# A four-layer attention network on one core: the causal layer's batches as one list of events, and two full layers in another order

## The chip, the cores and the metric

The kernel runs on one core of one Trainium2 chip. The metric is the device time of one execution in microseconds. The kernel before takes 1417.38 us (median of three runs, 1416.2 to 1417.79).

## The reference

The input x has four batches of 256 channels by 1024 tokens (32x32), all in fp32. It goes through four attention layers one behind the other, each with a residual.

```
x = L0(x)   # 4 batches: softmax(q k) over 1024 keys, q and k of 32 channels, values of 256; gamma * out + x
x = L1(x)   # group norm, q/k/v projections, softmax over 1024 keys, output projection, + x
x = L2(x)   # causal: layer norm, 8 heads of 32 channels over one shared k/v, output projection,
            # layer norm, then feed-forward: ln, w1, ln, gelu, w2, + residual
x = L3(x)   # as L1
```

L0, L1 and L3 are called full layers below, L2 the causal layer. Batches don't depend on each other; within a batch the layers do.

## The kernel before

One program holds two chains of work that share the engines. The full chain runs the twelve full layers in the order of the list `FULL` (L0, L1 and L3, four batches each). The causal chain runs L2 for batches 0 to 3. C0 to C3 are the causal layer of batches 0 to 3 here, L1.2 is L1 of batch 2.

Each chain is a generator on each engine, and the strings in `ORDER` say for each engine which chain takes the next step: digits, letters and F/C. On TensorE a digit (full) or a small letter (causal) also names the PSUM bank where the next unit is put. So the order of the work on each engine is written out by hand or by a search ahead of time, and each engine waits in that order.

Full layer: after the group norm (step gn: a small matmul, L756, then `h_hi` on ScalarE, `h_lo` on VectorE) come the queries q0 (L766), values, and for each of eight query tiles the scores (s, L685 or L716), the row maximum and 1/sum on VectorE, the exponents on ScalarE (L1045), the turned probabilities (t, 4 transposes each, L729, copied by ScalarE at L1058), and four value products o0 to o3 (L738). Product o2 needs turns up to t11, o3 up to t15. VectorE adds the result to the batch's tile (L1312).

Causal layer of one batch: opening (xt transposes of the input, L879; layer norm on VectorE with a root on GpSimd; xn transposes, q2, kv, vt; DMAs that stack q; max products, L951; shift, L908), then eight blocks of exponents (L968) and values (L987) with feed-forward pieces between them, then the rest: w2 of part 2 and all of part 3 (wo, ln2b, f1b, ta, w1, f2b, tg, w2). Feed-forward part 3 is a chain in which each piece needs the one ahead of it. Before the change `causal_schedule` lists these events for a single batch and each engine loops over the batches, so no event of batch b+1 can stand ahead of the last one of batch b:

```python
    tail = NQ - 2
    events += divide + pending + norm(K - 1) + [("tg", tail), ("w2", tail)]
    return events + [(e, tail + 1) for e in FEED_FORWARD]
```

Tiles are shared. Batch tiles are `x[0]`, `x[1]`, `x[0]`, `z` for L0 of batches 0 to 3, and `z`, `x[1]`, `x[0]`, `z` for L3. So the input of batch 3 (`z`) is loaded only when both stores of L3.0 have landed: SyncE issues store, store, load in that order (`stores`, L589; load L580), and its DMAs for the causal chain stand between them in one queue.

Of the kernel before, what the change touches and what calls it, by code (L numbers as in the profile page):

```python
# [8 lines left out]
ALU = mybir.AluOpType  # L9
# [3 lines left out]
P = 128  # L13
# [21 lines left out]
FULL = [("L0", 0), ("L1", 0), ("L0", 1), ("L1", 1), ("L0", 2), ("L3", 0), ("L1", 2), ("L0", 3), ("L1", 3), ("L3", 1),  # L35
        ("L3", 2), ("L3", 3)]
# [8 lines left out]
        "0Fc4F60F2Fe50F72d5F401F760FFF3F516F021FFF3F0215ga1FFF027FFF03F513F5F0246F012F405F710FFF2F456F012FFF3F5670b3F"  # L45
        "FF457FFFac4F6F0ce5F0F2h4F670F234gFahc601hFaFF4cgacFg7a6c0F457gcFcaefFcaFf1F3705gCgbegbCdhaC6fbdFaCfFcaFcCe76"
        "h6aFfFhabCceCbFhdfCbgda6fb1F3hfCC1dC6fCFb2eFgeC6bddC1fa3ahc5dFa7dC05hbFd7C03bCFfa7C56dhaFdCFadFahfc0cCFec624"
        "dFdCC6a23CeCFgCFaFbC3fCFac75a6d4C7aCFgFdCFaC76fC3CFCeFcFCa6F3F15F3Fh0c5F730FecCfd725F017FdFF5F20db3Fh156FFF2"
        "F701efec70bFhFFfcaeh67c6aFFhecaheFcaeaCbg0hgcCehaC1adFf3dCa5dfdC1F5dFh0ceh5c0dC4gFaC360Feh36ehC4aFgc0b67ecFF"
        "agCFC4cCFa7C62aF04f7fFcCeFcFcCe6acFef0123g4acFCgFhFa2C4dC4FgaFCFcga4gCca4F6ca6e1gFdC5Fbd3hfC1C3gC1dFC76f3CFb"  # L50
        "275FdCb7C34acFfhFCFaC3fF7a6C0FdC576aCFCCFhfF1FCa34706FhFFh017FgfFFCca6F4F2a6F4F2ah4F620Fd764F076bcaeFhFhF1F0"
        "7dfdfbca4F76da2aedgFaeFfF0F7eCcf34cf6aCchaC5FFgbdFaCg2d2adC2FfhFaFdedcCfaCecgaCebgdea2hgCCe0FC6cC4a6beFaC4aF"
        "ggCe0cgef6ca6aC2Fega74C0gCFc74cC2aeFgaC4g5a6cheFacCFeaF2egCCaFCeC60b4CgFc6C01eCcgFeFhCcCFa4bCFaCh3C72C0Cbf7F"
        "FFCg707FFFg7a3Fcb53Cfc0F4F6c04ch0Fc345F701F340fgbcFFbFh4F0cg1cgeca5Fhcace7aca10fFFhCdbF4agbCFahgC6320be6ceCa"
        "bFdbCFFdha52dhgaC7ebCdaFbfCdFafcdaFgfCCdChC0bf3Fa5aC5d0fFdC5Facch0ge2ac4C0hcF75dCcC3F750Fc475cCaeFcaCFcageca"
        "gCaFc6F23abCCaCfChCacCfCahc4F601cCdCafCcCaCFCCagFF4FCh63271FaFFa760FbcFFC74F026F4F0264F012F704F617FFF2F014F6"
# [36 lines left out]
NORM_PIECES = 3  # L93
LN_SLOTS = 4
# [63 lines left out]

def causal_schedule():

    events = [("xt", 0), ("xt", 1), ("xn", 0), ("q2", 0), ("kv", 0), ("vt", 0)]
    events += max_events(0) + max_events(1) + [("shift", 0), ("shift", 1)]
# [60 lines left out]
def causal_units():  # L223

    out = [("prep.vo1", "dve", 2), ("prep.qk1", "dve", 1), ("prep.b2", "dve", 1), ("prep.vo3", "dve", 2),
           ("prep.qk3", "dve", 1)]
    for b in range(B):
        for e in causal_schedule():
            if e[0] == "values":
                if is_final(e):  # L230
                    out.append((causal_name(b, e), "act", 1))
            elif e[0] not in NO_UNIT:
                out.append((causal_name(b, e), "act" if e[0] in FILLED_BY_ACT else "dve", causal_banks(e)))
    return out
# [7 lines left out]
def causal_openings():  # L242

    width = {u[0]: u[2] for u in causal_units()}
    out = [u for u in width if u[0] == "p"]
    for b in range(B):
        for e in causal_schedule():
            if e[0] not in NO_UNIT and (e[0] != "values" or e[2] == 0):
                out.append(causal_name(b, e))
    return [(name, width[name]) for name in out]  # L250
# [34 lines left out]
def build(nc, t):  # L285

    schedule = causal_schedule()
# [15 lines left out]
    norms = ["ln1.0", "ln1.1"]  # L303
    for e in schedule:
        if e[0] in ("wo", "ln2b", "w1"):
            norms.append("%s.%d" % ({"wo": "ln2", "ln2b": "f1", "w1": "f2"}[e[0]], e[1]))
    NORMS = len(norms)
    norm_no = {name: i for i, name in enumerate(norms)}
    ready = [("xt", 0), ("xt", 1)] + [e for e in schedule if e[0] in ("f1b", "f2b")]
    ready = [{"xt": ("xn", e[1]), "f1b": ("ta", e[1]), "f2b": ("tg", e[1])}[e[0]] for e in ready]  # L310
    READY = len(ready)
# [5 lines left out]
    with ExitStack() as ctx:  # L317
# [310 lines left out]
        def _(pool):  # L628
# [23 lines left out]
            def causal_chain():  # L652
                for b in range(B):
                    for name in norms[:2]:
                        root(b, name)
                        yield
# [14 lines left out]
        def _(pe):  # L671
# [320 lines left out]
            def causal_chain():  # L992
# [12 lines left out]
                for b in range(B):  # L1005
                    for e in schedule:
                        if e[0] in NO_UNIT:
                            continue
# [665 lines left out]
```

## Time and profile before

| | us |
|---|---|
| median of 3 runs | 1417.38 |
| profiled execution, its own time | 1414.86 |
| span of the profile | 1413.1 |
| TensorE busy | 1303.7 (92%) |
| VectorE busy | 866.2 (61%) |
| ScalarE busy | 594.1 (42%) |
| GpSimd busy | 93.9 (7%) |
| mean granted TensorE clock | 0.973 |

TensorE is busy for 92% of the span, and what is left is many short waits of at most a few microseconds. The granted clock is at one of two levels, 1.2 or 2.4 GHz (0.5 or 1.0 in the rows). In the rows a time in square brackets is how long the engine was idle ahead of the instruction, and behind it stands what ended that.

### The profile page before, as it was taken

The page shows a single profiled execution, that of the slowest core. Times are in us where ns is not written, and L with a number is a line of the kernel's source. Part 1 is how long each engine was busy: PE and PEld are TensorE (multiplying, and loading weights), DVE is VectorE, ACT ScalarE, POOL GpSimd, SP SyncE. Part 2 cuts the span into 40 slices and gives each one's busy share as a digit, 9 for nine tenths or more (in the row PEclk, how much of TensorE's full clock was granted, in tenths as well). Part 3 has the DMA queues.
Part 4 walks back from the last instruction along what each step waited for, and adds up shares of the span by engine and source line. Part 5 has one row for each costly group of instructions (what it writes and reads, how often), then busy time and mean ns, then how long its engine had stood idle before and what let it go on. Part 6 is the DMA issues. An engine that isn't in the chain of part 4 may idle for free.

```text
span 1413.1 us, 21791 instructions
## 1 busy us (share of the span) xinstructions
PE 1303.7 (92%) x8800; PEld 1018.9 (72%) x8800; DVE 866.2 (61%) x1854; ACT 594.1 (42%) x973; POOL 93.9 (7%) x134
## 2 busy tenths in 40 slices
PE   6889989989998989999999899899989999999898
PEld 5768776766767767777778767667778676767686
DVE  3534466767548759676545767775567587766442
ACT  3424344344445434434443543444434344454242
POOL 0000000100000001000000001100010011001000
PEclk9999999999999999999999999999999999999899
DMA  5000020000000100001000100000001001000000
GB/s 185 1 0 1 30 46 22 3 23 1 1 2 1 45 16 10 13 27 45 1 2 0 46 5 20 24 1 2 1 1 45 11 29 38 2 1 16 15 1 30
DMA packets 20610, 27.04 MB, mean 19 GB/s; under 512 B 3488, under 2 KB 14240, under 8 KB 20512
## 3 DMA queue, kind: packets, MB, share of 16 engines
q1 hardware_dynamic: 20512, 25.66, 6.5%
q8 instruction: 71, 1.16, 0.3%
q14 instruction: 27, 0.22, 0.1%
HBM read 8.61 MB, written 4.19 MB: 9 GB/s over the span
## 4 chain that ended last, share of the span: by engine, by line
PE 82%; DVE 7%; ACT 7%; issue 2%; SPq 1%; DMA 1%; POOL 0%; ACTq 0%; DVEq 0%
PE ring L685 26%; PE ring L738 25%; PE ring L987 9%; PE ring L951 5%; PE ring L968 5%; PE ring L729 4%; ACT probs L1045 2%; ACT probsT L1058 1%; PE ring L766 1%; PE ring L887 1%; ACT cprobs L1214 1%; DVE part_max L1573 1%; PE ring L955 1%; PE ring L920 1%; PE ring L772 1%
## 5 line engine op out<-in xcount | busy, mean ns | idle before, releaser
L738 PE MATMUL ring<-probsT,vt 128*128 128x256 f32 x1536 | 363.3, 387 | 16.9 <-ACT probsT L1058 16.0
L738 PEld LDWEIGHTS ring<-probsT,vt 128*128 128x128 f32 x1536 | 288.2, 193 | 67.4 <-ACT probsT L1058 19.9
L1214 ACT ACTIVATE cprobs<-ring 128x1024 f32<-128x1024 f32 (+1 forms) x160 | 150.5, 941 | 248.2 <-PE ring L968 247.7
L1045 ACT ACTIVATE probs<-ring,neg_max 128x1024 f32<-128x1024 f32 x96 | 107.1, 1116 | 163.4 <-DVE neg_max L1291 97.0
L1573 DVE TENSOR_REDUCE part_max<-ring 128x2 f32<-128x1024 f32 (+2 forms) x112 | 126.8, 1140 | 34.8 <-PE ring L951 22.8
L951 PE MATMUL ring<-ks,qs 96*128 96x512 f32 (+3 forms) x384 | 111.2, 388 | 13.8 <-ACT cprobs L1214 5.0
L1290 DVE TENSOR_REDUCE shift_max<-ring 128x1 f32<-128x1024 f32 x64 | 78.3, 1224 | 63.9 <-PE ring L685 62.3
L1058 ACT COPY probsT<-ring 128x512 f32<-128x512 f32 x192 | 102.3, 592 | 36.0 <-PE ring L729 36.0
L729 PE MATMUL ring<-consts,probs 128*128 128x128 f32 x768 | 105.9, 279 | 6.7 <-ACT probs L1045 3.7
L968 PE MATMUL ring<-qs,ks 98*128 98x512 f32 x288 | 106.6, 442 | 4.9 <-DVE h_lo L1258 2.4
L685 PE MATMUL ring<-h_hi,q_hi 128*128 128x512 f32 x256 | 106.9, 418 | 2.7 <-ACT probs L1045 1.4
L729 PEld LDWEIGHTS ring<-consts,probs 128*128 128x128 f32 x768 | 89.2, 143 | 26.2 <-issue 8.9
L685 PE MATMUL ring<-h_hi,q_lo 128*128 128x512 f32 x256 | 100.5, 392 | 0.0
L685 PE MATMUL ring<-h_lo,q_hi 128*128 128x512 f32 x256 | 100.2, 391 | 0.0
L987 PE MATMUL ring<-cprobs,v 128*32 128x256 f32 (+1 forms) x1280 | 95.9, 371 | 0.0
L987 PE MATMUL ring<-cprobs,ones 128*32 128x256 f32 (+1 forms) x1280 | 92.3, 360 | 0.0
L951 PEld LDWEIGHTS ring<-ks,qs 96*128 96x128 f32 x384 | 63.4, 197 | 37.3 <-issue 9.8
L649 POOL TENSOR_TENSOR rstd<-var_eps,half_neg 128x2 f32<-128x2 f32 (+1 forms) x56 | 46.2, 826 | 529.0 <-DVE var_eps L1471 529.0
L664 POOL TENSOR_SCALAR_AFFINE_SELECT cprobs<-cprobs 128x512 f32<-128x512 f32 x64 | 41.9, 655 | 558.1 <-ACT cprobs L1214 558.0
L1302 DVE TENSOR_SCALAR probs<-probs,row_inv 128x1024 f32<-128x1024 f32 x96 | 72.4, 754 | 3.4
L1594 DVE RECIPROCAL sums<-sums 128x128 f32<-128x128 f32 x64 | 57.8, 930 | 21.8 <-ACT nums L1223 21.5
L968 PEld LDWEIGHTS ring<-qs,ks 98*128 98x128 f32 x288 | 49.6, 192 | 25.9 <-issue 13.9
(221 smaller groups left out, 2136.4 us busy)
## 6 DMA issues: line engine op xcount, KB each, us to landing
qs<-q_hi SPq DMA_DIRECT2D x32, 128.0 KB, 2.3
qs<-q_hi SPq DMA_DIRECT2D x64, 64.0 KB, 2.0
x<-x_dram SPq DMA_DIRECT2D x3, 1024.0 KB, 5.7
qs<-q_lo SPq DMA_DIRECT2D x16, 128.0 KB, 2.3
qs<-max_rows SPq DMA_DIRECT2D x128, 2.0 KB
qs<-q_lo SPq DMA_DIRECT2D x32, 64.0 KB, 2.0
out_dram<-z SPq DMA_DIRECT2D x4, 512.0 KB, 2.8
out_dram<-x SPq DMA_DIRECT2D x4, 512.0 KB, 2.9
```

Source lines behind the costliest of these rows:

```text
L685: ins = mm(out, w, m, start=first and n == 0, stop=last and n == len(every) - 1)
L729: last = nc.tensor.transpose(o[:, j, :], probs[:, ti % 2, (TPH * hf + j) * P:(TPH * hf + j + 1) * P], ident)
L738: last = mm(o[:, ct * QUARTER:(ct + 1) * QUARTER], vt[:, j, ct * P:(ct + 1) * P], probsT[:, qi % (NQ - 1), j, :], start=j == 0, stop=j == ...
L951: last = mm(o, stack(k, a, 3 * DH, at, at + P), ks[0:3 * DH, lo:hi], start=i % own == 0, stop=not diag and i % own == own - 1)
L968: last = mm(heads(name)[:, a:a + own, 0:n], ks[0:3 * DH + 2, jt * P:(jt + 1) * P], stack(k, slice(a, a + own), 3 * DH + 2, QUARTER - n, QU ...
L987: last = mm(acc[DH * a:DH * (a + 1), (half + 1) * QUARTER - n:(half + 1) * QUARTER], w, causal_probs(step, n)[:, a, :], start=jt == 0 and ...
L1045: A(probs[:, ti % 2, :], flat(full_name(l, b, ("s", ti))), ACT.Exp, bias=neg_max[:, ti:ti + 1], accum_out=row_sum[:, ti:ti + 1]).then_inc( ...
L1058: nc.scalar.copy(probsT[:, ti // 2 % (NQ - 1), js, (ti % 2) * P:(ti % 2 + 1) * P], slot(name)[:, 0, :].rearrange("p (s n) -> p s n", n=P)) ...
L1214: A(causal_probs(step, n), heads(name)[:, :, 0:n], ACT.Exp).then_inc(read_done["c", "act"], 1)
L1290: full_then(v.tensor_reduce(shift_max[:, ti:ti + 1], flat(name), AX_X, ALU.max, negate=True))
L1302: v.tensor_scalar(probs[:, ti % 2, :], probs[:, ti % 2, :], row_inv[:, ti:ti + 1], None, ALU.mult).then_inc(probs_scaled["dve"], 1)
L1573: v.tensor_reduce(cols if ti < TPH else parts[:, ch, :], src[:, :, 0:n], AX_X, ALU.max, negate=True).then_inc(read_done["c", "dve"], 1)
```

## The change

Three things. The causal chain becomes one list of (batch, event) over all batches (`causal_order`), which all five engines follow. In it the first event of the next batch (`xt` 0) stands 6 events ahead of the end of the blocks, and the rest of the opening takes turns with the last feed-forward pieces by the table `TURNS`; `xt` 1 comes behind the last `w2`, since it writes `xs` tiles that this reads. In `FULL` L1.2 and L3.0 change places. All strings of `ORDER` are new. Layer-norm slots, the counts of the norms and of what has been normed are numbered over the list in place of batch by batch. No instruction is added or removed.

```diff
-FULL = [("L0", 0), ("L1", 0), ("L0", 1), ("L1", 1), ("L0", 2), ("L3", 0), ("L1", 2), ("L0", 3), ("L1", 3), ("L3", 1),
-        ("L3", 2), ("L3", 3)]
+FULL = [("L0", 0), ("L1", 0), ("L0", 1), ("L1", 1), ("L0", 2), ("L1", 2), ("L3", 0), ("L0", 3), ("L1", 3), ("L3", 1), ("L3", 2), ("L3", 3)]
...
     "PE": (
-        "0Fc4F60F2Fe50F72d5F401F760FFF3F516F021FFF3F0215ga1FFF027FFF03F513F5F0246F012F405F710FFF2F456F012FFF3F5670b3F"
+        "0Fc4F60F2Fe50F72d5F401F756FFF3F750F26d7FFF0F2675d4FFF017FFF05F204F6F2046F012F405F710FFF2F456F012FFF3F5670b3F"
...
+EARLY = 6
+TURNS = [(0, 1), (3, 2), (1, 0), (1, 1), (3, 2), (1, 2), (1, 2)]
...
+def opening():
+
+    return [("xn", 0), ("q2", 0), ("kv", 0), ("vt", 0)] + max_events(0) + max_events(1) + [("shift", 0), ("shift", 1)]
...
-    tail = NQ - 2
-    events += divide + pending + norm(K - 1) + [("tg", tail), ("w2", tail)]
-    return events + [(e, tail + 1) for e in FEED_FORWARD]
+    return events, divide + pending + norm(K - 1)
+
+
+def causal_order():
+
+    body, closing = causal_schedule()
+    last = NQ - 1
+    feed = [("tg", last - 1), ("w2", last - 1)] + [(e, last) for e in FEED_FORWARD]
+    out = [(0, ("xt", 0)), (0, ("xt", 1))] + [(0, e) for e in opening()]
+    for b in range(B):
+        here = [(b, e) for e in body]
+        if b < B - 1:
+            here.insert(len(here) - EARLY, (b + 1, ("xt", 0)))
+        out += here + [(b, e) for e in closing]
+        now, after = [(b, e) for e in feed], [(b + 1, e) for e in opening()] if b < B - 1 else []
+        for own in TURNS if after else ():
+            out += [now.pop(0) for _ in range(own[0])] + [after.pop(0) for _ in range(own[1])]
+        out += now + ([(b + 1, ("xt", 1))] if b < B - 1 else []) + after
+    return out
```

**Place 1: TensorE at the end of L3.2.** `consts,probs` is a turn of four transposes to each x4, `probsT,vt` x16 is a whole value product, the `ffw`/`hn` rows are w1 of C3's last part (12 matmuls), `consts,an` is ta or tg, `consts,xs` the first half of w2. Before:

```order
L729 MATMUL ring<-consts,probs 128x128 x16
L738 MATMUL ring<-probsT,vt 128x256 x8
L887 MATMUL ring<-consts,an 128x128 x4
L738 MATMUL ring<-probsT,vt 128x256 x8
L685 MATMUL ring<-ffw_hi,hn_hi 128x256
...
L729 MATMUL ring<-consts,probs 128x128 x8
L738 MATMUL ring<-probsT,vt 128x256 x8
```

and in the change, where the 12 rows of w1 stand between the turns and the value product, and 12 rows of w2 between the last two turns and the last product:

```order
L903 MATMUL ring<-consts,an 128x128 x4
L745 MATMUL ring<-consts,probs 128x128 x16
L701 MATMUL ring<-ffw_hi,hn_hi 128x256
...
L754 MATMUL ring<-probsT,vt 128x256 x12
L903 MATMUL ring<-consts,an 128x128 x4
L936 MATMUL ring<-consts,xs 128x128 x4
L754 MATMUL ring<-probsT,vt 128x256 x4
L745 MATMUL ring<-consts,probs 128x128 x8
L701 MATMUL ring<-act_hi,ffw_hi 128x256
...
L754 MATMUL ring<-probsT,vt 128x256 x16
```

What was in the middle of the value products (w1) or behind them (w2) now stands ahead of them.

**Place 2: ScalarE from the end of C0 to the start of C1.** `xs` is the copy of the input that opens a batch, `gelu` tg of parts 2 and 3, `cprobs` causal exponents, `sums` and `nums` the last block's result. Before, both copies stand behind the last w2 (`z`):

```order
L1193 ACTIVATE gelu_79<-ring,vecs 128x256 x2
L1045 ACT_TABLE_LOAD
L1045 ACTIVATE probs,row_sum<-ring,neg_max 128x1024
L1058 COPY probsT<-ring 128x4x128 x2
L1199 ACTIVATE z<-ring,vecs 128x256 x2
L1172 COPY xs<-ring 128x1024 x2
```

In the change the first copy stands ahead of the last exponents, q2 and kv (`q_hi`, `an`, `ks`) ahead of the last feed-forward part, and the second copy behind its w2:

```order
L1187 COPY xs<-ring 128x1024
L1228 ACTIVATE cprobs<-ring 128x1024
L1228 ACTIVATE cprobs<-ring 128x4x128
...
L1208 ACTIVATE gelu_78<-ring,vecs 128x256 x2
L1214 ACTIVATE z<-ring,vecs 128x256 x2
L1051 ACTIVATE q_hi<-ring,bq_129 128x512 x2
...
L1208 ACTIVATE gelu_79<-ring,vecs 128x256 x2
...
L1204 CAST max_rows<-ring 8x256 x2
L1187 COPY xs<-ring 128x1024
```

The opening's long chain has moved ahead by a whole feed-forward part, but its second half (`xs` again) has not.

**Place 3: TensorE at the start of C2, beside the end of L3.0.** `consts,x_49` x8 are the transposes xt 1, `consts,an` x8 xn 1, which needs the layer norm of what xt 1 brought. Before, with xt 0 and xt 1 together (x16) and xn 1 30 us and more behind them, the rows about xt were

```order
L685 MATMUL ring<-act_hi,ffw_lo 128x256
L879 MATMUL ring<-consts,x_49 128x128 x16
L685 MATMUL ring<-h_hi,wqk_hi 128x512
L685 MATMUL ring<-h_lo,wqk_hi 128x512
L685 MATMUL ring<-h_hi,wqk_lo 128x512
```

(the `wqk` rows open L0.3), and now

```order
L924 MATMUL ring<-consts,max_cols 8x128 x2
L895 MATMUL ring<-consts,x_49 128x128 x8
L745 MATMUL ring<-consts,probs 128x128 x8
L984 MATMUL ring<-qs,ks 128x512 x2
L754 MATMUL ring<-probsT,vt 128x256 x4
L903 MATMUL ring<-consts,an 128x128 x8
```

Between xt 1 and xn 1 only two turns, one exponent piece and a quarter of a value product are left.

## Rows read from the trace of the kernel before

**Rows 1.** The page, busy time by engine.

```profile
PE 1303.7 (92%) x8800; PEld 1018.9 (72%) x8800; DVE 866.2 (61%) x1854; ACT 594.1 (42%) x973; POOL 93.9 (7%) x134
```

**Rows 2.** Windows (busy PE, PEld, DVE, ACT, POOL; clock, DMA share, GB/s).

```profile
183.84:1330.50 1146.66, 1074.98 (x7607) 821.34 (x7607) 752.59 (x1619) 498.95 (x803) 90.16 (x124) 0.98 0.06 16
1330.50:1413.10 82.60, 72.06 (x362) 61.97 (x362) 30.12 (x56) 26.84 (x49) 0.69 (x1) 0.93 0.04 13
```

**Rows 3.** Windows of TensorE (busy, clock, DMA) at half clock; the sum of eleven.

```profile
241.60:245.00 3.40, 3.40 (x35) 0.51 0.45 109
289.40:296.30 6.90, 6.17 (x17) 0.51 0.00 0
...
1187.10:1193.90 6.80, 6.07 (x14) 0.50 0.08 19
...
sum 54.70, PE 50.31; mean PE 4.57
```

**Rows 4.** Timeline of TensorE: the first queries of L1.1, L1.2, L3.1, L3.2.

```profile
290.13 0.76 PE L766 MATMUL ring<-h_hi,L_wqk_hi 128*128 128x512 f32 x1 [2.56 <-ACT h_hi L1104]
...
659.81 0.47 PE L766 MATMUL ring<-h_hi,L_wqk_hi 128*128 128x512 f32 x1 [1.36 <-ACT h_hi L1104]
...
1044.55 0.47 PE L766 MATMUL ring<-h_hi,L_wqk_hi 128*128 128x512 f32 x1 [1.73 <-issue]
...
1187.83 0.76 PE L766 MATMUL ring<-h_hi,L_wqk_hi 128*128 128x512 f32 x1 [3.29 <-issue]
```

**Rows 5.** Timeline of TensorE: o2 and o3 of L1.2.

```profile
753.79 0.80 PE L738 MATMUL ring<-probsT,vt 128*128 128x256 f32 x1 [2.72 <-ACT probsT L1058]
...
766.02 0.48 PE L738 MATMUL ring<-probsT,vt 128*128 128x256 f32 x1 [0.73 <-ACT probsT L1058]
```

**Rows 6.** Timeline of TensorE: waits from C0's end into C1.

```profile
451.74 0.33 PE L887 MATMUL ring<-consts,an 128*128 128x128 f32 x1 [1.92 <-DVE an L1487]
...
454.70 0.39 PE L685 MATMUL ring<-act_hi,ffw_hi 128*128 128x256 f32 x1 [1.41 <-DVE act_lo L1552]
...
520.56 0.38 PE L908 MATMUL ring<-consts,max_cols 128*8 128x128 f32 x2 [2.04 <-DVE max_cols L1584]
...
526.79 0.41 PE L901 MATMUL ring<-consts,an 128*128 128x128 f32 x2 [1.54 <-ACT cprobs L1214]
```

**Rows 7.** Timeline, C1: its xt transposes, and VectorE's norm that xn waits for.

```profile
456.23 1.91 PE L879 MATMUL ring<-consts,x 128*128 128x128 f32 x16
...
462.64 1.37 DVE L1487 TENSOR_SCALAR an<-xs,ln_mv,rstd 128x256 f32<-128x256 f32 x4
```

**Rows 8.** Timeline, the end of L3.0 and the reload of z for L0.3.

```profile
653.40 0.88 DVE L1312 SCALAR_TENSOR_TENSOR z<-ring,L_bvo,z 128x256 f32<-128x256 f32 x2 [3.43 <-PE ring L738]
654.30 0.38 SPq L589 DMA_DIRECT2D out_dram<-z  x1
657.10 0.39 SPq L580 DMA_DIRECT2D z<-x_dram  x1
683.09 2.42 SPq L612 DMA_DIRECT2D qs<-max_rows  x4
...
765.85 2.00 ACT L1091 CAST h_hi<-z 128x1024 fp32r<-128x1024 f32 x2
...
775.36 1.21 DVE L1380 TENSOR_TENSOR h_lo<-z,h_hi 128x1024 fp32r<-128x1024 f32 x1
```

**Rows 9.** DMA issues: KB, median us from issue to landing.

```profile
out_dram<-z SPq DMA_DIRECT2D x4, 512.0 KB, 2.8
z<-x_dram SPq DMA_DIRECT2D x1, 1024.0 KB, 4.9
```

**Rows 10.** Windows, all engines: 30 us about the end of C0.

```profile
450.00:480.00 30.00, 24.16 (x146) 20.77 (x147) 24.04 (x59) 17.15 (x29) 2.83 (x3) 1.00 0.07 15
```

**Rows 11.** Timeline of TensorE: a short wait ahead of a half-clock stretch.

```profile
240.65 0.33 PE L901 MATMUL ring<-consts,an 128*128 128x128 f32 x1 [1.38 <-DVE ks L1260]
```

More of the change, by code:

```diff
@@ L226, in causal_units @@
            ("prep.qk3", "dve", 1)]
[L227 to L233, printed above, removed]
+    for b, e in causal_order():
+        if e[0] == "values":
+            if is_final(e):
+                out.append((causal_name(b, e), "act", 1))
+        elif e[0] not in NO_UNIT:
+            out.append((causal_name(b, e), "act" if e[0] in FILLED_BY_ACT else "dve", causal_banks(e)))
     return out
@@ L245, in causal_openings @@
     out = [u for u in width if u[0] == "p"]
[L246 to L249, printed above, removed]
+    for b, e in causal_order():
+        if e[0] not in NO_UNIT and (e[0] != "values" or e[2] == 0):
+            out.append(causal_name(b, e))
     return [(name, width[name]) for name in out]
@@ L285, in build @@
 def build(nc, t):
-    schedule = causal_schedule()
+    order = causal_order()
+    schedule = [e for b, e in order if b == 0]
     units = {"f": full_units(), "c": causal_units()}
@@ L301, in build @@
     hi_no = {**numbered("f", ("q", "k")), **numbered("c", ("xn", "q2", "q", "kv", "ta"))}
[L303 to L311, printed above, removed]
+    norm_of = {"xt": "ln1", "wo": "ln2", "ln2b": "f1", "w1": "f2"}
+    norms = [(b, f"{norm_of[e[0]]}.{e[1]}") for b, e in order if e[0] in norm_of]
+    norm_no = {norm: i for i, norm in enumerate(norms)}
+    turned_by = {"xt": "xn", "f1b": "ta", "f2b": "tg"}
+    normed = [(b, (turned_by[e[0]], e[1])) for b, e in order if e[0] in turned_by]
+    normed_no = {turn: i + 1 for i, turn in enumerate(normed)}
     diagonal = [e for e in schedule if e[0] == "exp" and e[2] >= TPQ * BLOCKS[e[1]][1]]
@@ L1460, in norm_start @@
             def norm_start(b, name, src, t0, n, gain=None):
[L1462 removed]
+                s = norm_no[b, name] % LN_SLOTS
                 for i in range(n):
@@ L1612, in causal_chain @@
                     yield from prepare(l)
-                for b in range(B):
-                    for e in schedule:
-                        if e[0] == "max":
-                            causal_max(b, e)
-                        elif e[0] == "norm":
-                            normalise(b, e)
-                        elif len(e) == 2 and e[0] != "shift":
-                            yield from stage(b, e)
-                            continue
-                        else:
-                            continue
-                        yield
+                for b, e in order:
+                    if e[0] == "max":
+                        causal_max(b, e)
+                    elif e[0] == "norm":
+                        normalise(b, e)
+                    elif len(e) == 2 and e[0] != "shift":
+                        yield from stage(b, e)
+                        continue
+                    else:
+                        continue
+                    yield
             weave(ORDER["DVE"], full_chain(), causal_chain())
```

175 lines of the change are left out of this document (84 added, 91 removed).

## The prediction

> **What bounds the kernel now.** I read the busy times of the page first: TensorE is busy for 1303.7 of 1413.1 us, VectorE for 866, the others for less [rows 1]. So TensorE bounds, and since the change adds and removes no instruction on it, the time can only move by what TensorE waits and by the clock it is granted. Then the windows. TensorE's order is the same up to the second batch's start and from the group norm of L3.3 to the end; both keep their waits. Between them lies a stretch of 1146.7 us with TensorE busy for 1075.0 [rows 2], so 71.7 us idle: that, and the clock inside it, is all that the new order can touch. The last 82.6 us lose 10.5 in the same way and are kept [rows 2].
>
> The clock next. In eleven stretches of this middle part, 54.7 us together, the granted clock reads 0.5, so 1.2 in place of 2.4 GHz [rows 3]. At half clock a matmul takes twice as long, so these stretches cost up to 27 us, more than a third of the idle time again. They begin within about a microsecond of a wait: the one at 289.4 about the wait of 2.56 us that ends at 290.13, the one at 1187.1 about that of 3.29 [rows 3, 4], another about the 2.72 us ahead of o2 of L1.2 [rows 5], but one also behind a mere 1.38 us [rows 3, 11], while 1.92 and 1.41 us close to each other brought none [rows 6, 10]. A removed wait of two or three microseconds is thus often worth its length and 1.7 to 3.4 us more.
>
> **How I count a wait.** For a handoff (a matmul, work on other engines, a matmul that needs it) I add up the TensorE work that stands between the two in its order: the cover. Cover plus wait in the trace is what the handoff needs. In the new order I take the new cover from the need. Pieces have their undisturbed length from the trace: 12 matmuls of 128x256 take 1.53 us (454.70 to 456.23 [rows 6, 7]), a turn 0.44, an exponent piece 0.55, a quarter of a value product 1.6.
>
> **Starts of full layers.** The first queries wait for h_hi, about 3.3 to 5.3 us behind the group-norm matmul: covers of 1.35, 2.28, 1.52 and 1.99 and the waits 2.56, 1.36, 1.73 and 3.29 of L1.1, L1.2, L3.1 and L3.2, 8.9 in all [rows 4]. The covers are now 4.04, 2.65, 5.44 and 2.68: 0, 1.0, 0 and 1.8 are left (for L3.2 between its own need of 5.3 and the usual 3.7). L3.0 goes from 5.50 to 2.91 and L1.3 from 4.04 to 1.66, which brings 0.8 and 1.5 more. Sum: -3.8.
>
> **Ends of full layers.** o2 waits for the copy of turn t11, need 0.87 + 2.72 = 3.6 us, and o3 waits 0.73 [rows 5]; L3.2 repeats both numbers within 0.01. Place 1 of the change puts 12 matmuls of w1 ahead of o2 and 12 of w2 ahead of o3. The cover of o2 is then 2.4 in L3.2 and 3.8 in L1.2, that of o3 1.5 in both. Of 6.9 us 1.2 stay. Sum: -5.7.
>
> **From C0 to C1.** Four waits, 6.9 us [rows 6]: tg of part 3 (cover 1.81, now 2.85, need 3.7), w2 (0.81, now 2.3, need 2.2), shift of block 3 (0, now 3.2, need 2.0), vt 1 (1.8, now 2.8, need 3.3). 1.4 us are left. Sum: -5.5.
>
> **From C1 to C2, a new wait.** The transposes xn need the norm of what xt brought. In C1 VectorE ends it at 464.0, and the first eight of the 16 transposes end at about 457.3 [rows 7]: 6.7 us. So far xn 1 stood 30 us or more behind xt 1 and never waited. At place 3 the cover is 3.0 us, so TensorE waits 3.7; behind it in its order stand the max products of blocks 2 and 3 and o2 of L3.0. In C1 and C3 the cover is 8 and 9.6. vt 1 of C2 loses 0.9. Sum: +4.6.
>
> **The reload of z.** L0.3 now follows straight behind L3.0, whose tile it reuses; before, a whole layer lay between (load at 657, copied at 766 [rows 8]). The path: residual 0.9 us, store 2.8, load 4.9 [rows 8, 9], half of the h_hi copy 1.0, h_lo 1.2 [rows 8]: 10.8. SyncE also issues six stacking DMAs between store and load, 0.6 each by the four of 2.42 us [rows 8], which together with the store's own 0.4 outlast it by 1.2: 12.0 us. Between the last product of L3.0 and the first query of L0.3 stand 14.0 us of causal work. I take 0. If that cover failed, every microsecond of lateness would be paid, with half clock on top; even with the store landing in twice its time (5.6 us) the wait would be 0.8 us, and with the load too in twice its time 5.7, the bound from above.
>
> **The rest of the 71.7 us.** 49 us are waits in the middle of layers, reshuffled by the new strings. I counted cover and usual need for all handoffs of this stretch in both orders: 73.6 us of shortage before (the trace has 71.7 idle) and 57.7 now, and places short by 1.3 us or more fall from 23 to 9. That is -15.9, of which the parts above make -10.4; I trust two thirds of the remainder: -3.5. The same count laid VectorE's instructions with their mean durations against each 30 us of TensorE's work: before four such stretches ask VectorE for over 30 us (37.3, 33.3, 30.9, 30.5), now two do, by at most 0.8.
>
> **Clock.** The waits removed or cut at L1.1, L1.2's end, L3.2's start and end and C1's shift each have a half-clock stretch: 6.9, 3.4, 6.8, 3.4 and 3.5 us, 24.0 together, half of it lost: -12.0. At L3.2 a wait of 1.8 may keep half of its stretch, +1.7, and the new wait at xn 1 brings one of 3.4 to 6.8, +2.6. Sum: -7.7.
>
> **Sum.** -3.8 - 5.7 - 5.5 + 4.6 - 3.5 - 7.7 = -21.6 us against the profiled execution's own 1414.86, so 1393.3. Its median lies 2.5 above that execution, so I forecast 1396 us for the median.
>
> **Rivals.**
> *Short waits hold the clock down.* The waits go by 13.9 us but the half-clock stretches only change their places, since one of them follows a wait of only 1.38 us [rows 3, 11] and of such waits dozens stay. Against it: eight of the eleven stand at waits of 1.8 us or more. 1417.4 - 13.9 = 1404 us. By the Trainium skill, page "TensorE: Matmul & The Clock Gate", section "A second HAM failure mode: psum-queue depth-cycling", short idle times between groups of matmuls are enough to make the clock swing; taken strictly the clock term would be 0 here. No row rules it out, and the wait of 1.38 us speaks for it.
>
> *The waits only move.* Every engine takes its work in the written order, and a wait removed on TensorE lets the next producer be late: the 71.7 us stay and so do the half-clock stretches. 1417 us. Against it: the count of shortage, which comes within 2 us of the old trace's 71.7 and falls by 16 in the new order.
>
> *Slower: VectorE at the batch boundaries.* In each boundary some 13 links of two serial chains (opening and last feed-forward part) now share VectorE with the full layer's softmax. Already before, in 30 us about the end of C0 VectorE was busy 24.0 and TensorE only 24.2 [rows 10]. If each link of 13 x 3 is late by 1 us beyond its cover, that is 39 us: 1396 + 39 = 1435 us. It decides from (21.6 + 2.8) / 39 = 0.6 us a link. Against it: VectorE's demand falls exactly where it was highest.
>
> *More than that.* The rest comes in full (-5.5) and the clock returns in most of the eleven stretches (-20): 1414.9 - 10.4 - 5.5 - 20 + 2.5 = 1381 us.
>
> **How the numbers follow.** Chances: forecast 0.55 (its own range 1386 to 1403 us, from the need at xn 1 and L3.2 and the clock), short waits hold the clock 0.17, more 0.05, waits only move 0.09, slower 0.14. Measurement can't tell less than 0.2% (2.8 us) from no change. Faster 0.77, same 0.09, slower 0.14. The range leaves out the slower case and the far end of "more": 1382 to 1415 us.
>
> **What would show it.** In the profile after: no wait of 2.7 us ahead of L738 at the ends of L1.2 and L3.2; first queries of L1.1 and L3.1 with no wait; a wait of some 4 us ahead of the xn transposes (line of `an`) at about half of the span, with half clock behind it; no wait for `z` or h_lo at the start of L0.3; TensorE's mean clock up from 0.973 to about 0.98; idle time of TensorE down from 109 to about 95 us. Wrong it would be if waits of 1 to 2 us multiply where VectorE is named as releaser, or if L0.3 starts late behind its load.

## The result

The change takes 1402.01 us (median of four runs, 1398.08 to 1403.89) where the kernel before takes 1417.59 (four runs, 1416.2 to 1418.3). The ratio is 0.9888, its 95% interval 0.9863 to 0.9912: 1.1% faster. The forecast was 1396 us, its range 1382 to 1415.

The profiled execution took 1400.56 us, against 1414.86 before. Its busy times, from the page:

```profile
span 1398.8 us, 21787 instructions
PE 1298.5 (93%) x8800; PEld 1015.2 (73%) x8800; DVE 867.1 (62%) x1854; ACT 594.0 (42%) x973; POOL 92.4 (7%) x134
```

Then the windows of the middle and of the end (span of the stretch, busy PE, PEld, DVE, ACT, POOL, clock, DMA share, GB/s). They hold the same 7607 and 362 matmuls as those of before:

```profile
183.84:1315.96 1132.12, 1070.75 (x7607) 818.80 (x7607) 753.36 (x1619) 498.91 (x803) 88.63 (x124) 0.98 0.06 16
1315.96:1398.80 82.84, 72.40 (x362) 61.97 (x362) 30.12 (x56) 26.84 (x49) 0.70 (x1) 0.95 0.05 20
```

The whole gain is in the middle: 1132.12 in place of 1146.66 us [rows 2]. It splits in two. The time in which TensorE does nothing falls from 71.7 to 61.4 us, 10.3. The time in which it is busy falls from 1074.98 to 1070.75, 4.2; since it is the same matmuls, that is the clock (in one profile of each kernel; the timed runs are compared further down). The forecast had 13.9 for the waits and 7.7 for the clock.

The places that the prediction named, in the timeline of TensorE after (start, duration, in brackets the idle time ahead):

```profile
288.79 0.59 PE L924 MATMUL ring<-consts,max_cols 128*8 128x128 f32 x2 [2.90 <-DVE max_cols L1598]
...
295.39 0.47 PE L782 MATMUL ring<-h_hi,L_wqk_hi 128*128 128x512 f32 x1 [0.71 <-issue]
...
452.80 0.66 PE L903 MATMUL ring<-consts,an 128*128 128x128 f32 x4 [0.93 <-DVE an L1501]
...
457.20 0.38 PE L701 MATMUL ring<-act_hi,ffw_hi 128*128 128x256 f32 x1 [0.76 <-DVE act_lo L1566]
...
481.86 0.71 PE L984 MATMUL ring<-qs,ks 98*128 98x512 f32 x2 [2.58 <-ACT probs L1060]
...
659.36 0.48 PE L782 MATMUL ring<-h_hi,L_wqk_hi 128*128 128x512 f32 x1 [2.56 <-ACT h_hi L1119]
...
761.93 0.73 PE L984 MATMUL ring<-qs,ks 98*128 98x512 f32 x2 [1.55 <-DMA qs<-max_rows]
764.08 1.22 PE L754 MATMUL ring<-probsT,vt 128*128 128x256 f32 x2 [1.42 <-ACT probsT L1073]
...
1053.21 0.47 PE L782 MATMUL ring<-h_hi,L_wqk_hi 128*128 128x512 f32 x1 [1.07 <-issue]
...
1187.71 0.47 PE L782 MATMUL ring<-h_hi,L_wqk_hi 128*128 128x512 f32 x1 [0.74 <-issue]
```

Both halves count. The first queries of L1.1, L3.1 and L3.2 (rows at 295.39, 1053.21, 1187.71) wait 0.7 to 1.1 us where they waited 1.7 to 3.3 [rows 4]. But one unit ahead of L1.1's queries the shift of block 5 of C0 now waits 2.90, L3.0's queries have a wait of 2.56, and exp 1.0 of C1 (the first exponent unit of block 1) one of 2.58 that was not there. At the ends of L1.2 and L3.2 the waits of 2.72 and 0.73 [rows 5] are gone altogether.

### The profile page after: what moved, and what is told of

It is laid out like the page before. It is cut to its first block, busy times and chain, and to the rows that moved or that the text cites. A ratio compares the mean times of both kernels' runs of the same rounds, so it can differ in the third digit from the quotient of the medians.

```text
span 1398.8 us, 21787 instructions
## 1 busy us (share of the span) xinstructions
PE 1298.5 (93%) x8800; PEld 1015.2 (73%) x8800; DVE 867.1 (62%) x1854; ACT 594.0 (42%) x973; POOL 92.4 (7%) x134
## 4 chain that ended last, share of the span: by engine, by line
PE 82%; DVE 9%; ACT 5%; issue 2%; DMA 1%; SPq 0%; POOL 0%; ACTq 0%; DVEq 0%
PE ring L701 28%; PE ring L754 25%; PE ring L1003 9%; PE ring L984 5%; PE ring L967 4%; PE ring L745 4%; PE ring L903 1%; DVE part_max L1587 1%; ACT probs L1060 1%; ACT cprobs L1228 1%; PE ring L936 1%; PE ring L782 1%; DVE cmax L1587 1%; DVE neg_max L1301 1%; PE ring L971 1%
## 5 line engine op out<-in xcount | busy, mean ns | idle before, releaser
L754 PE MATMUL ring<-probsT,vt 128*128 128x256 f32 x1536 | 358.9, 386 | 8.7 <-ACT probsT L1073 8.4
L967 PE MATMUL ring<-ks,qs 96*128 96x512 f32 (+3 forms) x384 | 108.3, 379 | 11.5 <-ACT cprobs L1228 5.7
L701 PE MATMUL ring<-h_lo,q_hi 128*128 128x512 f32 x256 | 100.3, 392 | 0.0
L701 PEld LDWEIGHTS ring<-h_hi,q_hi 128*128 128x128 f32 x256 | 48.1, 188 | 19.9 <-issue 6.4
```

What stands on the lines that cost most here:

```text
L701: ins = mm(out, w, m, start=first and n == 0, stop=last and n == len(every) - 1)
L754: last = mm(o[:, ct * QUARTER:(ct + 1) * QUARTER], vt[:, j, ct * P:(ct + 1) * P], probsT[:, qi % (NQ - 1), j, :], start=j == 0, stop=j == ...
L967: last = mm(o, stack(k, a, 3 * DH, at, at + P), ks[0:3 * DH, lo:hi], start=i % own == 0, stop=not diag and i % own == own - 1)
```

## Experiments

**Which stretch of the order brings how much.** There are two places at which both orders have done the same work on every engine: the last w2 of part 2 of C0 and that of C2. Cut there, the strings of before and of the change can be mixed; up to some 25 units behind a cut use other PSUM banks, since the two orders leave other banks free. The edit in short form, `change` and `before` standing for the strings of the two kernels, for `s1_front` (change up to the first cut; `s4_middle` is before, change, before; `s2_back` is before, before, change):

```diff
-    "PE": change,  "DVE": change,  "ACT": change,  "POOL": change,  "SP": change
+    "PE": change[:363] + before[363:],  "DVE": change[:233] + before[233:],  "ACT": change[:200] + before[200:],
+    "POOL": change[:27] + before[27:],  "SP": change[:20] + before[20:]
...
+INTERLEAVED = []        # the batch boundaries b to b + 1 that take turns; [0, 1] in s4_middle, [2] in s2_back
...
+        if b < B - 1 and b not in INTERLEAVED:
+            out += now + [(b + 1, ("xt", 0)), (b + 1, ("xt", 1))] + after
+            continue
```

`FULL` is new in `s4_middle` alone.

> Every engine follows the order of the change up to the last w2 of C0's part 2, and the order of before from there on: of the change only the reshuffle of L0.1 and L1.1 is in it, no taking turns and the old list of full layers. In the traces of before and of the change the same 1769 matmul instructions end at 412.7 and at 408.6 us, so if what is won in a stretch stays won, this kernel ends 4.0 us earlier than before: 1413.6 us, with the first query of L1.1 waiting about 0.7 us. Rival, the waits only move: the 4 us are given back in C0's end, 1417 us.

> The order of before up to the same place near C0's end, then the change up to the last w2 of C2's part 2, then before again: it holds the boundaries C0 to C1 and C1 to C2 with their taking turns, and the changed places of L1.2 and L3.0. By the two traces this stretch takes 596.99 us before and 594.55 in the change: 2.4 us, so 1415.2. My prediction had for the same parts -5.5 (C0 to C1), -2.9 (end of L1.2), +4.6 (xn 1) and half clock about even: also about 1414. Rival, these boundaries carry the gain and the front only lays the ground for it: 1410 or less.

> The order of before up to the last w2 of C2's part 2, then that of the change: the boundary C2 to C3 and L3.1 to L3.3. By the two traces the change takes 8.0 us less from there to the end (before 1009.7 of 1413.1, change 1003.2 of 1398.8): 1409.6 us. Rival, the waits only move: 1415 to 1417.

Measured, against 1416.53 for the kernel before (23 runs beside these, 1411.15 to 1418.71):

| | median us (runs, lowest to highest) | ratio, 95% interval | expected |
|---|---|---|---|
| s1_front | 1415.55 (12, 1410.19 to 1417.08) | 0.9986 (0.9974 to 0.9998) | 1413.6 |
| s4_middle | 1414.21 (12, 1405.33 to 1417.27) | 0.9970 (0.9950 to 0.9990) | 1415.2 |
| s2_back | 1408.97 (5, 1408.80 to 1415.34) | 0.9954 (0.9941 to 0.9967) | 1409.6 |

The ratios multiply to 0.991, the change has 0.989. By the medians alone half of the gain would lie in the last third (C2 to C3, L3.1 to L3.3), and the two boundaries and the exchange of L1.2 and L3.0 would bring little. But a median carries the clock as well as the waits: `s1_front` brought 1 us where the traces had promised 4. The windows tell the two apart. They show the stretch between the two cuts, with TensorE's busy time and clock. In the kernel before:

```profile
412.67:1009.66 596.99, 561.30 (x3950) 0.98 0.06 15
```

in `s4_middle`, which has the order of the change there:

```profile
412.92:1001.38 588.46, 557.81 (x3951) 0.98 0.06 16
```

in the change itself:

```profile
408.65:1003.20 594.55, 563.89 (x3948) 0.97 0.06 15
```

and in `s1_front`, which has the order of before there:

```profile
411.49:1014.96 603.47, 567.91 (x3950) 0.97 0.06 15
```

Between `s4_middle` and the change the order is the same there and so are the waits: idle 30.65 and 30.66 us. But the same matmuls are busy for 557.8 in one and 563.9 in the other, since the half-clock stretches in them add up to 20.4 and 34.0 us. In the same way the kernel before took 597.0 us for this stretch (half clock 23.8), and `s1_front` and `s2_back`, with its order and the same waits, both 603.5 (40.8). Six microseconds thus come and go with no change in the order at all. The twelve timed runs of `s4_middle` fall in two groups: five of 1405 to 1409 us at a clock of 0.970 to 0.976, seven of 1414 to 1417 at 0.962 to 0.968. My reading of 4.0 us for the front from two single profiles was of this kind: half-clock stretches add up to 30.6 us there in the profile of before and to 17.0 in that of the change, but to 27.2 in `s1_front`, which has the change's order up to the cut.

So the parts are to be read by TensorE's idle time. Between the cuts it is 35.7 us in the kernel before (35.6 in `s1_front` and `s2_back`) and 30.7 in the change. From the second cut to the group norm of L3.3 it falls from 19.7 to 14.9, and to 16.0 in `s2_back`, as these windows of before, the change and `s2_back` show:

```profile
1009.66:1330.50 320.84, 301.18 (x2150) 0.98 0.06 18
```

```profile
1003.20:1315.96 312.76, 297.88 (x2150) 0.99 0.06 16
```

```profile
1016.48:1330.61 314.13, 298.16 (x2151) 0.99 0.06 16
```

Ahead of the first cut it goes from 16.3 to 15.8. Of the 10.3 us of waits, the front thus brings 0.5, the two boundaries with the exchange 5.0 and the last third 4.8. Runs at the same clock say the same: at 0.973 `s4_middle` has 1406.51 us and the kernel before 1413.93 to 1416.98, at 0.975 `s2_back` has 1408.87 and 1408.97 and the kernel before 1411.15 and 1411.77. That both medians came within 1 us of what I had expected is luck. In `s4_middle` a lower clock (0.969 on average against 0.972) took back most of what the waits had given, in `s2_back` a higher one (0.974) added to it, and its own profiled execution took 1415.34.

The cuts also show what removed the waits at the ends of layers. `s4_middle` has no wait at the end of L1.2 and still 2.73 us ahead of o2 of L3.2, `s2_back` has 2.72 at L1.2 and none at L3.2, and `s1_front` has both. Each wait goes where the order about it is changed, and only there.

**What holds the start of L0.3.** The prediction had no wait there; the trace after has 2.18 us. SyncE and VectorE were the suspects. `r1_store` moves SyncE's store and load of `z` forward:

```diff
-        "FCCCCCCCCCCCCCCCCCCCCCCCCCCCCCCFCCCCCFCFCCCCCCCCCCCCCCCFCCCFCCFFFF"),
+        "FCCCCCCCCCCCCCCCCCCCCCCCCCCCCCCFCCCFCFCCCCCCCCCCCCCCCCCCFCCCFCCFFFF"),
```

> The change, with SyncE's second store of L3.0 issued ahead of the four shift DMAs and the load of z ahead of the twelve stacking DMAs, that now stand between. Theory A, VectorE holds the start of L0.3: h_lo stands in VectorE's order behind the two maxima of block 4 (to 813.05) and the last half of a norm (0.9), and starts when they end, at 813.87, 3.4 us after the first half of h_hi: the wait of 2.18 us ahead of L0.3's first projection stays as it is, 1402 us. Theory B, the reload is late because SyncE issued the store 6.1 us after the residual: the wait goes, and with it 1.7 to 3.4 us of the half clock at 814: 1397 to 1399 us.

Measured: 1401.37 us (1396.3 to 1403.97), and the wait is unchanged. In its timeline SyncE stores at once and loads 2.9 us later (in the change the store comes 6.1 us after the residual and the load 4.8 behind it). VectorE does the maxima first, and h_lo behind them, though the load was issued 14 us before the maxima:

```profile
795.94 0.38 SPq L608 DMA_DIRECT2D out_dram<-z  x1
...
798.88 0.40 SPq L599 DMA_DIRECT2D z<-x_dram  x1
...
813.16 2.36 DVE L1587 TENSOR_REDUCE part_max<-ring 128x2 f32<-128x1024 f32 x2
816.34 2.36 DVE L1394 TENSOR_TENSOR h_lo<-z,h_hi 128x1024 fp32r<-128x1024 f32 x2
...
817.72 0.47 PE L701 MATMUL ring<-h_hi,wqk_hi 128*128 128x512 f32 x1 [2.19 <-DVE h_lo L1394]
```

`r2_hlo_first` leaves SyncE alone and moves one letter of VectorE's string, so that the first half of h_lo stands ahead of the two maxima:

```diff
-  ...CCCCCCCCCCCCCCFFCCCCFCFFFFFC...
+  ...CCCCCCCCCCCFCCCFCCCCFCFFFFFC...
```

> The change, with the first half of h_lo of L0.3 ahead of the two maxima of block 4 in VectorE's order, and nothing else. Theory A (VectorE's queue holds L0.3's start): h_lo starts when h_hi is done, about 810.6 in place of 813.87, and the wait of 2.18 us ahead of L0.3's first projection goes to 0; the maxima come 1.2 us later, which may cost up to that behind the projection. Theory B (the load is late): the wait stays at 2 us. In the time: 1400 to 1402.

Measured: 1399.38 us (1397.38 to 1400.93), ratio to before 0.9880 (0.9864 to 0.9897). In time that can't be told from the change (0.9888). In its timeline h_lo starts at 810.97, 0.15 us behind the first half of h_hi. The projection waits 0.40 us, with another 0.52 ahead of it, so 1.3 of the 2.18 us are gone and not all:

```profile
810.97 1.22 DVE L1394 TENSOR_TENSOR h_lo<-z,h_hi 128x1024 fp32r<-128x1024 f32 x1
812.11 2.35 DVE L1587 TENSOR_REDUCE part_max<-ring 128x2 f32<-128x1024 f32 x2
...
813.38 0.73 PE L967 MATMUL ring<-ks,qs 96*128 96x512 f32 x2 [0.52 <-DVE part_max L1587]
814.51 0.76 PE L701 MATMUL ring<-h_hi,wqk_hi 128*128 128x512 f32 x1 [0.40 <-DVE part_max L1587]
```

So the 2.18 us were VectorE's written order. But the reload has little room. In the change its load, issued at 804.40, takes 5.1 us to land, so it lands at 809.5, and ScalarE starts h_hi at 809.51, after 0.1 us of standing idle for it. `g4_fitted_hlo` below shows what comes when TensorE is earlier.

**Does half clock come from standing still?** If it does, it must go when TensorE is kept busy in the same waits. `f1_filled` does that to the change and `f2_before_filled` to the kernel before. The added matmuls write to the bank that the unit is about to open and are overwritten by its first matmul with `start=True`; the number for each place is its wait, less some 0.2 us, divided by 0.128 us (12 matmuls of that size take 1.53 us [rows 6, 7]).

```diff
+COVER = {"L1.0.gn0": 19, "L1.0.q0": 27, "C0.exp.1.0.2.2": 15, "C0.shift5": 21, "C1.exp.1.0.2.2": 18,
+         "L3.0.q0": 18, "C2.exp.0.0.0.0": 10, "L3.0.o2": 9, "C2.vt1": 12, "C2.wo0": 10, "L0.3.q0": 15,
+         "C2.shift6": 21, "C3.vt0": 9, "C2.tg3": 8, "L3.3.gn0": 12, "L3.3.q0": 27, "L3.3.o2": 14}
...
+            def cover(name):
+                for _ in range(COVER.get(name, 0)):
+                    mm(slot(name)[:, 0, 0:C], wqk0[0][:, 0, 0, :], wv0[0][:, 0, :], start=True, stop=True)
...
-                pe.wait_ge(h_hi, 2 * n + 1)
                 o = open_unit(full_name(l, b, ("q", 0)))
+                cover(full_name(l, b, ("q", 0)))
+                pe.wait_ge(h_hi, 2 * n + 1)
```

> The change, with matmuls whose result is thrown away in front of 17 of TensorE's waits for other engines (1.3 us or longer, 37.5 us together): each is given as many 128x256 matmuls of a constant, 0.128 us each, as fit into its wait, written to the bank that the next unit opens with start. Nothing else moves, and the waits still end when their producers are done. Theory A, half clock comes because TensorE stands still: 12 of the 14 half-clock stretches of the profile after the change lie at these waits, about 57 us, half of it lost: up to 28 us come back, 1374 to 1385 us. Theory B, the clock changes whatever TensorE does: 1402 us. Theory C, the added matmuls are late themselves: above 1402.

> The kernel before, with the same added matmuls in front of 17 of its waits (gn and q0 of L1.0, vt1 of C0, q0 of L1.1, tg3 of C0, shift3 and vt1 of C1, q0 and o2 of L1.2, shift5 of C2, gn and q0 of L3.1, q0 and o2 of L3.2, gn, q0 and o2 of L3.3). Theory A: some 52 us of its half clock lie at these, 26 us come back, about 1391 us; the distance to the filled change is then the difference of the idle times alone, about 10 us. Theory B: 1417.

Measured: `f1_filled` 1388.97 us (1386.42 to 1390.64), ratio to before 0.9807 (0.9790 to 0.9824), and all its runs at a clock of 0.993 or 0.994. `f2_before_filled` 1408.47 (1402.76 to 1409.65), 0.9938 (0.9921 to 0.9956), clock 0.987 to 0.991. Windows about the start of L1.0 and of L3.3 show it best; both have two waits each (gn and q0). In the change:

```profile
86.69:98.31 11.62, 5.30 (x17) 0.71 0.00 0
1314.22:1324.32 10.10, 4.76 (x17) 0.83 0.14 52
```

and in `f1_filled`, the same steps with 46 and 39 more matmuls, over in 1.9 and 1.4 us less:

```profile
86.15:95.85 9.70, 9.01 (x63) 1.00 0.00 0
1305.58:1314.31 8.73, 8.19 (x55) 1.00 0.16 60
```

TensorE does more than three times the matmuls in less time, because the useful ones run at 2.4 GHz and not in part at 1.2. The half-clock stretches of the whole program fall from thirteen and a rest at the end (64.1 us) to five and a rest at the end (22.0 us). Two of the five lie where the added matmuls stood behind the wait (216.8, 479.7), the others at waits of 0.6 to 1.2 us that were not filled:

```profile
193.00:199.80 6.80, 6.80 (x34) 0.50 0.01 2
216.80:220.20 3.40, 3.40 (x17) 0.51 0.02 7
479.70:483.10 3.40, 3.38 (x16) 0.50 0.02 5
547.90:551.30 3.40, 3.40 (x21) 0.51 0.00 0
1176.00:1179.40 3.40, 3.40 (x22) 0.50 0.00 0
```

Theory A holds, but the size was off: 13 us came back in the change, not 17 to 28. In the two profiles the 265 added matmuls cost an estimated 33.9 us of work (0.128 each), idle time falls from 100.3 to 71.7, and the old matmuls are busy for 1281.6 us in place of 1298.5: 33.9 - 28.6 - 16.9 = -11.6, which is the difference of the spans. The expectation had overlooked three things. Five stretches stayed or came anew. Part of a half-clock stretch is itself waiting and costs nothing (in the stretch at 90.7 TensorE is busy for 4.1 of 6.8 us). And at three places the added matmuls stood behind the real wait, as this timeline of `f1_filled` at exp 1.0 of C0 shows, where the wait is for the bank:

```profile
216.57 3.35 PE L703 MATMUL ring<-wv_hi,wqk_hi 128*128 128x256 f32 x15 [1.90 <-ACT probs L1079]
```

The kernel before missed by more: 7 us came back and not 26. Its profiled execution is the fastest of its six runs, so the profile can't say why the others took longer. The distance between the two filled kernels is 19.5 us, where I had expected the 10 of the idle times alone; with `g2_before_fitted` and `g1_fitted` below it is 16.0.

**Mending that.** `g1_fitted` and `g2_before_fitted` take out the misplaced matmuls, `g4_fitted_hlo` adds the VectorE order of `r2_hlo_first`, and `g3_half_filled` has half as many at each place. The edit of `g1_fitted` against `f1_filled`, of the list only the entries that differ:

```diff
-"C0.exp.1.0.2.2": 15, "C1.exp.1.0.2.2": 18, "C3.vt0": 9, "L3.0.q0": 18, "C0.shift5": 21, "C2.exp.0.0.0.0": 10, "L3.0.o2": 9
+"L3.0.q0": 9, "C0.shift5": 20, "C2.exp.0.0.0.0": 9, "L3.0.o2": 8
```

> The filled change again, but without the added matmuls at the three places where TensorE waited for the bank itself, so that they stood behind the wait and not in it (exp 1.0 of C0 and of C1, vt 0 of C3), and with half of them at q0 of L3.0. In the trace of the filled change the extra matmuls there made the gap 3.0, 3.6, 0.8 and 0.9 us longer, and tg 3 behind them 0.9. If time is work plus idle plus half of the work at half clock, these 9.2 us come off and the clock stays: 1380 us. Rival, the saved time turns into other waits, since the full chain was ahead by it: 1385 to 1389.

> The filled kernel before, without the added matmuls at vt 1 of C1 and o2 of L3.3, and with fewer at q0 of L1.1 and gn of L3.1, where they stood behind the wait. 4.6 us come off: 1404 us. Both kernels then lose little by the clock, and their distance shows the waits that can't be filled: before keeps five half-clock stretches at unfilled waits (24.8 us), the change five (22.0).

> As the fitted change, but with half as many added matmuls at each place: TensorE still stands still at each, for 0.6 to 1.9 us. Theory A, any standing still of a microsecond is enough for half clock: most of the 12 stretches return, 1395 to 1400 us. Theory B, the length of the standing still decides and 2 us are needed: none returns, 1380 us. By the profiles so far, where 1.0 to 1.4 us had a stretch at some places and in some kernels and not in others, I expect between the two, 1388.

> The fitted change, and the first half of h_lo of L0.3 ahead of the two maxima in VectorE's order, without added matmuls at L0.3's first projection, since there is nothing left to wait for. The wait of 2.18 us goes: 1378 us, the best version. If the maxima that come 1.2 us later delay what follows, 1380.

| | median us (runs) | ratio to before, 95% interval | clock | expected |
|---|---|---|---|---|
| g1_fitted | 1388.54 (4) | 0.9805 (0.9777 to 0.9833) | 0.989 to 0.994 | 1380 |
| g2_before_fitted | 1404.51 (6) | 0.9919 (0.9898 to 0.9940) | 0.985 to 0.988 | 1404 |
| g3_half_filled | 1391.76 (6) | 0.9825 (0.9794 to 0.9856) | 0.980 to 0.991 | 1388 |
| g4_fitted_hlo | 1389.82 (5) | 0.9818 (0.9791 to 0.9845) | 0.988 to 0.992 | 1378 |

`g1_fitted` missed. The 9 us did not come off, and its time can't be told from that of `f1_filled` (0.9805 and 0.9807 of before); it lies in the range of the rival, 1385 to 1389. At the two places the gap got shorter as expected, but its profile has 33.5 us of half clock where `f1_filled` has 22.0 (10.2 us of it about 545 and 6.8 at 480, both at waits that both kernels have), and idle 75.9 where that has 71.7; 1.9 of these 4.2 us are its first wait for a load, some 2 are three waits (0.83, 0.72, 0.59) that the longer gaps had covered. `g2_before_fitted` came as expected. In the two fitted profiles idle time and added work together (246 and 211 matmuls at 0.128 us) are 113.6 us in `g2_before_fitted` and 102.9 in `g1_fitted`: the 10.7 us of waits between the two orders stay, with most of the half clock gone from both.

`g4_fitted_hlo` missed as well, and its timeline names the reason: here the reload is late. The load lands only at about 807.2. ScalarE stands idle for it for 2.23 us and VectorE for h_hi for 2.13, the maxima come behind h_lo, and TensorE waits for the bank that they have to read first:

```profile
802.12 0.58 SPq L602 DMA_DIRECT2D z<-x_dram  x1
...
807.21 1.99 ACT L1125 CAST h_hi<-z 128x1024 fp32r<-128x1024 f32 x2 [2.23 <-DMA z<-x_dram]
...
808.36 1.22 DVE L1413 TENSOR_TENSOR h_lo<-z,h_hi 128x1024 fp32r<-128x1024 f32 x1 [2.13 <-ACT h_hi L1125]
...
810.78 0.73 PE L985 MATMUL ring<-ks,qs 96*128 96x512 f32 x2 [2.60 <-DVE part_max L1606]
811.91 0.50 PE L709 MATMUL ring<-h_hi,wqk_hi 128*128 128x512 f32 x1 [0.40 <-DVE part_max L1606]
```

In `r2_hlo_first` the same order had cost 0.52 + 0.40 us, since TensorE came to this place 3.1 us behind the load's landing and here comes 1.0 behind it. `g4_fitted_hlo` with SyncE's order of `r1_store` would tell whether the wait goes once both are mended; it was not run.

`g3_half_filled` has its six runs in two groups, three of 1385.6 to 1388.2 at 0.990 or 0.991 and three of 1395.3 to 1395.7 at 0.980 or 0.981. It bears out neither theory. In its profile, what is left of the waits at L1.0 (1.57 and 1.98 us) and at L3.3 (1.02 and 1.91) brings no half clock, and that at gn of L1.3 and the shift behind it (1.05 and 1.52) does. Of its five stretches two lie at filled places (this one and C2's tg 3, 1.58 us), so most did not return, against theory A; and all but one stand at waits of less than 2 us, against theory B.

## Why the prediction came out as it did

Its sign and its range were right, its middle 6 us too low: by the profiles 3.6 us too much for the waits and 3.5 for the clock, while the medians lie 15.6 us apart and the profiles 14.3. Term by term; the waits by the trace of before and after:

| term | forecast | measured |
|---|---|---|
| starts of full layers (q0 of L1.1, L1.2, L3.1, L3.2, L3.0, L1.3) | -3.8 | 9.5 to 5.1: -4.4 |
| ends of L1.2 and L3.2 | -5.7 | 6.9 to 0: -6.9 |
| C0 to C1, four waits | -5.5 | 6.9 to 1.8: -5.1 |
| C1 to C2, xn 1 and vt 1 | +4.6 | 1.55 + 1.42 and +0.8: +3.8 |
| reload of z | 0 | +2.2 |
| rest | -3.5 | +0.1: the terms above make -10.4, all waits -10.3 |
| clock | -7.7 | -4.2 in the middle |

**Right, by its own reasoning:** the ends and starts of full layers and the boundary C0 to C1. Cover plus wait gives what a handoff needs, and the new cover subtracts from it: L3.2's o2 and o3, L3.1's and L3.2's queries and the four waits of C0 to C1 came within 1.2 us of what was written. L3.0 (0.8 more forecast, 2.6 measured) and L1.3 (1.5 more forecast, 0.5 less measured) were each off by about 2, in opposite directions, so that the row of the starts comes out well partly by luck.

**C1 to C2: the size right by luck, the place wrong.** xn 1 does not wait. In the timeline after, VectorE ends `an` at 765.51, 6.0 us after xt 1 (the need was put at 6.7), but TensorE comes to xn 1 only at 767.66, because exp 0.0 and o2 of L3.0 just ahead of it wait for 2.97 us. Exp 0.0 waits for the shift rows of block 0. They are the first four of eight DMAs that SyncE issues in a row, about 0.62 us each:

```profile
758.36 4.92 SPq L631 DMA_DIRECT2D qs<-max_rows  x8
```

The fourth is issued by 760.85 and lands at 761.9, and exp 0.0 starts at 761.93; the four of shift 1 stand behind and don't hold it. These four issues and the landing were not in my count. The forecast's wait at xn 1 and the measured ones ahead of it have different causes.

**Reload of z: 0 forecast, 2.2 measured, and the path mis-sized.** From L3.0's last product (ended 792.5) the path was put at 12.0 us and the cover at 14.0. SyncE issued the store only 6.1 us after the residual, behind four shift and six stacking DMAs, and the load landed at 809.5. With h_hi's and h_lo's first halves behind it (1.05 and 1.2 us) the path ends at an estimated 811.8, after 19.3 us. TensorE came for it at 813.06, after 20.5 us, of which 4.0 were waits of its own. So the path was covered by 1.3 us, and by luck; in `g4_fitted_hlo` it was not. What failed besides is the sentence that the reload is all that L0.3's start can wait for: VectorE's maxima and a norm stood ahead of h_lo, and `r1_store` and `r2_hlo_first` tell the two apart.

**The rest, -3.5: wrong, +0.1 measured.** The count of shortage took cover on TensorE against a usual need, and so gave each producer its usual time. Where VectorE is full, the need is longer and the wait comes back at another unit. The clearest case is L1.1's start. Its queries' wait goes from 2.56 to 0.71, but the shift of block 5, now one unit ahead, waits 2.90 for maxima that VectorE works off with nothing idle between; its timeline after:

```profile
284.90 1.22 DVE L1587 TENSOR_REDUCE part_max<-ring 128x2 f32<-128x1024 f32 x1
286.04 0.94 DVE L1608 RECIPROCAL sums<-sums 128x128 f32<-128x128 f32 x1
286.89 1.16 DVE L1587 TENSOR_REDUCE part_max<-ring 128x4 f32<-128x1024 f32 x1
288.09 0.16 DVE L1591 TENSOR_TENSOR cmax<-part_max 128x4 f32<-128x4 f32 x1
288.29 0.17 DVE L1596 CAST cmax_hi<-cmax 128x8 fp32r<-128x8 f32 x1
288.49 0.17 DVE L1597 COPY max_cols<-cmax_hi 128x8 f32<-128x8 f32 x1
288.57 0.16 DVE L1598 TENSOR_TENSOR max_cols<-cmax,cmax_hi 128x8 f32<-128x8 f32 x1
```

Exp 1.0 of C0 and C1 (2.07 and 2.58 us, new; the first takes the place of a wait of 2.45 us one exponent unit ahead) wait for a bank that ScalarE still reads; banks were not in the count either. The rival "the waits only move" was right for this term, and the idle times of the parts show that it was wrong for the whole.

**Clock, -7.7: right in mechanism, too large.** That waits bring half clock is shown by `f1_filled` and `f2_before_filled`. What failed is the step that a removed wait takes its stretch with it for good. The stretches at C1's shift, L1.2's end and L3.2's start and end did go, and that at L1.1's start went from 6.8 to 3.4 us, to the shift ahead of it. But other waits of 1.4 to 2.6 us brought stretches (217, 483, 661, 763, 814; the first stands for one at 214 before), and which of the many short ones brings one differs between profiles of the same order. The size is borne out by the timed runs: the mean clock is 0.976 in the change (four runs) and 0.972 in the kernel before (45 runs of the experiments), which comes to about 12 us less of half clock and so to 6 us at most. The rival that short waits hold the clock down had 1404 us, 2 from the result, and with the clock term at 0; the truth lies between it and the forecast. By the Trainium skill, page "TensorE: Matmul & The Clock Gate", section "A second HAM failure mode: psum-queue depth-cycling", short idle times between groups of matmuls make the clock swing. The runs here agree: filled, the change's mean clock goes from 0.976 (four runs) to 0.994 (five), and in `f1_filled` stretches stand at waits of only 1.21 us (547.9) and 0.99 us (1176.0).

**Slower, by VectorE at the boundaries:** its mechanism is real (it holds the shift of block 5 of C0 and L0.3's start; a shift of C2 waits 2.88 us, but one of C2 waited 2.90 before), its price of 1 us a link was far too high.

## What to carry over

Where each engine takes its work in a written order, count the cover of a handoff on the engine that waits, but take the need from the queue of the producer: what stands ahead of the result there, the SyncE DMAs and the reader of the bank too. A wait that vanishes in front of one unit should be looked for one unit ahead.

Compare two kernels, and the parts of one, first by their idle time, which between the cuts agreed within 0.2 us for the same order, and only then by busy time, which carries the clock. A single profile can't price a change of 4 us when the clock moves 6 by itself.

On a kernel that TensorE bounds, throw-away matmuls in a wait that can't be removed can pay: they took the change from 1402 to 1389 us, and the kernel before from 1415 to 1405 (`g2_before_fitted`). Where they stood behind the wait they made the gap longer, but to take them out there brought nothing that the time shows.

## What I had not expected of the hardware

The half-clock stretches of the thirteen profiles, but for the rests at the end, are 3.4, 6.8 or 10.2 us long, and the same wait, equal to a hundredth of a microsecond, doesn't bring the same in all kernels: the queries of L3.2, 3.29 us, have 6.8 us of it before and 3.4 in `s1_front` and `s4_middle`; vt 1 of C2, 1.77 us, has 3.4 in the change and in `r1_store` and none in `s4_middle`; o2 of L3.2, 2.72 us, has 3.4 before and in `s4_middle` and none in `s1_front`. One kernel's runs can fall in two groups 8 to 9 us apart for it (`s4_middle`, `g3_half_filled`). Why a run takes one or the other is not settled here.
